# A seven-product output projection: kept weight sums, and the hand-over from attention

## What is computed

```python
B, S, HID = (4, 128, 512)
D, HQ, HK = (128, 32, 8)
Wo = jax.random.normal(ks[4], (HID, HQ * D), jnp.float32) * 0.02
```

## Time and profile before

| what | value |
| --- | --- |
| median of 3 runs | 3381.02 us (3380.08 to 3381.89) |
| the profiled execution | 3377.51 us |
| its span | 3375.7 us, 70348 instructions |
| TensorE busy | 3244.6 us (96%) |
| VectorE, ScalarE, POOL busy | 2498.1, 1839.9, 1649.2 us |
| granted TensorE clock, mean | 0.985 |
| DMA | 647.5 MB, mean 192 GB/s |
| attention | to about 2883.6 us |
| projection | 2888.2 to about 3211.3 us |

### The profile page before, as it was taken

How to read it: one execution, slowest core, us unless ns; L and a number is a source line. 1 busy time by engine, 2 the same in 40 slices (tenths; PEclk the granted TensorE clock), 3 DMA queues, 4 the chain that set the end, 5 groups by cost and what they waited for, 6 DMA issues and landing times. The chain is left out here.

```text
span 3375.7 us, 70348 instructions
## 1 busy us (share of the span) xinstructions
PE 3244.6 (96%) x22206; PEld 2992.9 (89%) x22206; DVE 2498.1 (74%) x6389; ACT 1839.9 (55%) x4523; POOL 1649.2 (49%) x2754
## 2 busy tenths in 40 slices
PE   7799999999899999999899999999999999899899
PEld 5688899987778888888899999999999999788778
DVE  6445544445477777878899999989999998688884
ACT  4323322233227877888666666666666666555432
POOL 0231100000007878788677878767777776055302
PEclk9899999999999999999999999999999999899999
DMA  5412422334545554556776777767777777688753
GB/s 208 136 58 72 126 81 82 86 105 135 198 160 170 178 172 167 186 185 199 244 240 237 243 233 242 238 198 241 241 237 233 240 246 273 215 319 312 252 181 107
DMA packets 401100, 647.50 MB, mean 192 GB/s; under 512 B 41754, under 2 KB 267866, under 8 KB 383835
## 3 DMA queue, kind: packets, MB, share of 16 engines
q1 hardware_dynamic: 381018, 504.58, 44.5%
q0 software_dynamic: 19712, 138.42, 12.6%
HBM read 444.93 MB, written 197.92 MB: 190 GB/s over the span
## 5 line engine op out<-in xcount | busy, mean ns | idle before, releaser
L2657 PE MATMUL l2a_x<-l2a_pt,l2a_V 128*128 128x128 f32 x4096 | 545.0, 276 | 10.9 <-issue 8.9
L2657 PEld LDWEIGHTS l2a_x<-l2a_pt,l2a_V 128*128 128x128 f32 x4096 | 500.2, 193 | 13.5 <-issue 12.7
L2569 DVE CUSTOM_DVE_ANT_0 l2a_sm<-l2a_s,l2a_B 128x544 f32<-128x544 f32 x512 | 366.7, 716 | 63.2 <-PE l2a_s L199 55.6
L2523 ACT ACTIVATE l2a_p<-l2a_sm,l2a_st 128x544 f32<-128x544 f32 x512 | 380.0, 742 | 30.6 <-DVE l2a_st L2569 30.3
L2346 POOL CAST keys<-cache 128x256 fp32r x750 | 302.4, 451 | 184.1 <-issue 175.7
L2508 ACT ACTIVATE l2a_pt<-l2a_t 128x512 f32<-128x512 f32 x512 | 305.5, 597 | 101.1 <-PE l2a_t L2640 97.6
L2346 POOL CAST l2a_K<-cache 128x256 fp32r x768 | 306.8, 448 | 13.9 <-issue 6.3
L2640 PE MATMUL l2a_t<-ident,l2a_p 128*128 128x128 f32 x2048 | 307.7, 273 | 5.2 <-ACT l2a_quads L2516 5.2
L2581 DVE TENSOR_SCALAR l2a_p<-l2a_p,l2a_st 128x512 f32<-128x512 f32 x512 | 295.3, 577 | 18.2
L2069 POOL MEMSET l2q_eps<- 128x5 f32 x1 | 0.1, 103 | 622.8 <-DMA s_x<-moe_xr 622.8
L2516 ACT ACTIVATE l2a_quads<-l2a_x 128x128 f32<-128x128 f32 x512 | 142.0, 277 | 293.2 <-PE l2a_x L2658 293.2
(11 more groups left out here) (1033 smaller groups left out, 9074.0 us busy)
## 6 DMA issues: line engine op xcount, KB each, us to landing
s_qT<-l2q_qo SPq DMA_DIRECT2D x128, 512.0 KB, 2.8
part<-s_ao SPq DMA_DIRECT2D x28, 2048.0 KB, 9.3
head<-s_qT SPq DMA_DIRECT2D x64, 512.0 KB, 6.1
l2a_Q<-s_qT SPq DMA_DIRECT2D x64, 512.0 KB
s_ao<-l2a_combos SPq DMA_DIRECT2D x64, 512.0 KB, 4.5
s_ao<-l2a_quads SPq DMA_DIRECT2D x64, 384.0 KB, 2.5
s_kn<-l2q_ko SPq DMA_DIRECT2D x128, 128.0 KB
head<-s_kn SPq DMA_DIRECT2D x32, 512.0 KB, 5.9
```

The source lines that it names most:

```text
L2523: act.activation(prr[sc % 6][:, :].rearrange("p (k g j) -> p g k j", k=4, j=8), smr[sc % 2][:, :].rearrange("p (g k j) -> p g k j", k=4, j ...
L2569: dve.tensor_tensor_reduce(out=smr[sc % 2][:, :], in0=ps_s[sc % 2][:, 224:768], in1=Br[g % 2][:, :], scale=-SCALE, scalar=3e38, op0=ALU.ad ...
L2657: pe.matmul(px[:, P:256], V[:, k * D + hg * P:k * D + hg * P + P], pt[:, k, :], start=k == 0, stop=False)
```

## The change

Three edits.

**Kept sums.** The sum that POOL makes for product 3, B1 + B2 - B3, is stored by SP to a new buffer `s_wo_sum` in HBM, one store of 128 KB a step (`keep`). Product 6 loads block 0 and that sum, two DMAs of 128 KB, instead of the four blocks, and POOL makes one difference instead of three sums. A raw buffer whose sum is being stored is only loaded anew when the store has landed (`kept`).

**First parts.** The first three parts are asked for in pass `U - 2` of attention's loop instead of `U - 5`.

**Last combinations.** `combine` and `store_combos` are handed to `l2_out`, which makes and stores the last four combinations at its own start. `quads` and `combos` are allocated first in `l2_attn`, and `o` first in `l2_out`, over them. The order of blocks in `quads` is changed, so that one instruction of 128x512 makes t1 and t3 together; `quads` is then stored with two DMAs (two blocks and one).

```diff
@@ l2_attn
+    quads = st.slots("quads", 2, [P, 4, 256], each=2)
+    combos = st.slots("combos", 1, [P, 4, 256])
...
+    def store_combos(sp, k):
+        sp.wait_ge(combined, 3 * k + 3)
+        sp.dma_start(pair_at(k)[:, 3:7, :], combos[k][:, :, :]).then_inc(combos.sem(k), 16)
+
+    def combine(pool, k):
+        q, c = quads[k], combos[k]
+        pool.wait_ge(o_copied, 8 * k + 8)
+        if k:
+            pool.wait_ge(*combos.landed(k - 1))
+        pool.tensor_tensor(c[:, 0:2, :], q[:, 2:4, :], q[:, 1:3, :], ALU.subtract).then_inc(combined, 1)
+        pool.wait_ge(combined, 3 * k + 1)
+        pool.tensor_tensor(c[:, 2, :], q[:, 3, :], c[:, 0, :], ALU.subtract).then_inc(combined, 1)
+        pool.wait_ge(combined, 3 * k + 2)
+        pool.tensor_tensor(c[:, 3, :], q[:, 0, :], c[:, 2, :], ALU.subtract).then_inc(combined, 1)
...
-                    sp.dma_start(pair_at(k)[:, 0:3, :], quads[k][:, 0:3, :]).then_inc(quads.sem(k), 16)
+                    sp.dma_start(pair_at(k)[:, 0:2, :], quads[k][:, 0:2, :]).then_inc(quads.sem(k), 16)
+                    sp.dma_start(pair_at(k)[:, 2, :], quads[k][:, 3, :]).then_inc(quads.sem(k), 16)
...
-                    if sc == U - 5:
+                    if sc == U - 2:
...
-            store_combos(G // 2 - 1)
...
-            combine(G // 2 - 1)
@@ l2_out
-    sums_of = (0, 0, 2, 1, 1, 3, 0)
+    sums_of = (0, 0, 2, 1, 1, 1, 0)
...
                     if s >= 8 + NA:
                         sp.wait_ge(w_lo, s - NA + 1)
-                    a, z = blocks_of[p]
-                    sp.dma_start(raw_of(s), A["wo4"][k, :, a:z, :]).then_inc(raw_in[(s - 8) % NA], 16)
+                        if steps[s - NA][0] == 2:
+                            sp.wait_ge(kept[steps[s - NA][1] % 4], 16 * (steps[s - NA][1] // 4 + 1))
+                    if p == 5:
+                        sp.dma_start(raw_of(s)[:, 0, :], A["wo4"][k, :, 0, :]).then_inc(raw_in[(s - 8) % NA], 16)
+                        sp.dma_start(raw_of(s)[:, 1, :], S["wo_sum"][k]).then_inc(raw_in[(s - 8) % NA], 16)
+                    else:
+                        a, z = blocks_of[p]
+                        sp.dma_start(raw_of(s), A["wo4"][k, :, a:z, :]).then_inc(raw_in[(s - 8) % NA], 16)
+
+            def keep(s):
+                p, k, _ = steps[s]
+                if p == 2:
+                    sp.wait_ge(raw_summed, sums_at[s + 1])
+                    sp.dma_start(S["wo_sum"][k], raw_of(s)[:, 0, :]).then_inc(kept[k % 4], 16)
...
             parts.fetch(sp, 3)
+            store_combos(sp, uses - 1)
             sp.wait_ge(*before_c.landed(uses - 1))
             blocks.fetch(sp)
             for s, (p, k, ns) in enumerate(steps):
+                keep(s)
                 if s >= 8:
                     raw(s + NA)
...
-                    for h in range(2):
-                        sp.wait_ge(d_sems[h][0], 16)
+                    for z in (*d_sems[0], d_sems[1][0]):
+                        sp.wait_ge(z, 16)
...
+            combine(pool, uses - 1)
...
                     if p == 5:
-                        pool.tensor_tensor(r[:, 0, :], r[:, 0, :], r[:, 3, :], ALU.add).then_inc(raw_summed, 1)
-                        pool.tensor_tensor(r[:, 1, :], r[:, 1, :], r[:, 2, :], ALU.add).then_inc(raw_summed, 1)
-                        pool.wait_ge(raw_summed, sums_at[s] + 2)
                         pool.tensor_tensor(r[:, 0, :], r[:, 0, :], r[:, 1, :], ALU.subtract).then_inc(raw_summed, 1)
```

More of the change, by code:

```diff
@@ L2298, in l2_attn @@
     Br = [st.sb(f"B{i}", [P, KV]) for i in range(2)]
-    quads = st.slots("quads", 2, [P, 4, 256])
-    combos = st.slots("combos", 1, [P, 4, 256])
     ps_s = [st.ps(f"s{i}", [P, 1024]) for i in range(2)]
@@ L2356, in l2_attn, with pair_at @@
     fill = {1: 15, 2: 8, 4: 10, U // 2: 30}
+    def pair_at(k):
+        half, m = divmod(k, NB // 2)
+        return S["ao"][half, m // 2, :, :, m % 2, :]
+    def store_combos(sp, k):
[11 more added lines that the diff above has]
+        pool.tensor_tensor(c[:, 3, :], q[:, 0, :], c[:, 2, :], ALU.subtract).then_inc(combined, 1)
     def units(i):
@@ L2391, in fetch_new_values @@
                                  S["vn"][b * 32:(b + 1) * 32, (4 * half + h) * P:(4 * half + h + 1) * P]).then_inc(Nr.sem(g), 16)
-            def pair_at(k):
-                half, m = divmod(k, NB // 2)
-                return S["ao"][half, m // 2, :, :, m % 2, :]
-            def store_combos(k):
-                sp.wait_ge(combined, 4 * k + 4)
-                sp.dma_start(pair_at(k)[:, 3:7, :], combos[k][:, :, :]).then_inc(combos.sem(k), 16)
             sp.dma_start(iota[:, :], A["keypos"]).then_inc(iota_in, 16)
@@ L2455, in values @@
                                         bass.IndirectOffsetOnAxis(ap=rows[:, half, b:b + 1], axis=0)).then_inc(Vr.sem(g), 16)
-            def combine(k):
-                b11, b21, b22, b12 = (quads[k][:, e, :] for e in range(4))
-                t1, t2, t3, t4 = (combos[k][:, e, :] for e in range(4))
-                pool.wait_ge(o_copied, 8 * k + 8)
-                if k:
-                    pool.wait_ge(*combos.landed(k - 1))
-                pool.tensor_tensor(t1, b12, b11, ALU.subtract).then_inc(combined, 1)
-                pool.tensor_tensor(t3, b22, b12, ALU.subtract).then_inc(combined, 1)
-                pool.wait_ge(combined, 4 * k + 1)
-                pool.tensor_tensor(t2, b22, t1, ALU.subtract).then_inc(combined, 1)
-                pool.wait_ge(combined, 4 * k + 3)
-                pool.tensor_tensor(t4, b21, t2, ALU.subtract).then_inc(combined, 1)
             values(0)
@@ L2660, in l2_attn @@
     before.marks.close()
-    S["ao_stores"] = quads, combos, G // 2
+    S["ao_stores"] = quads, combos, G // 2, combine, store_combos
     return st
@@ L2708, in l2_out @@
     st = Stage(nc, "l2o")
+    o = [st.sb(f"o{h}", [P, 2, 2, 16, 2, 32]) for h in (1, 0)][::-1]
     ident, _ = S["ident"]
@@ L2719, in l2_out @@
     raw_in = [st.sem(f"wr{i}") for i in range(NA)]
+    kept = [st.sem(f"kept{i}") for i in range(4)]
     wp = [st.pair(f"w{i}", [P, 256]) for i in range(4)]
     bp = [st.pair(f"b{i}", [P, D]) for i in range(6)]
-    o = [st.sb(f"o{h}", [P, 2, 2, 16, 2, 32]) for h in range(2)]
     dr = st.slots("dr", 3, [P, D])
@@ L2750, in l2_out @@
     ends.update({max(s for s, z in enumerate(steps) if z[0] == p): (p, None) for p in range(1, 6)})
+    landings = [0] * N
+    for s in range(8, N):
+        landings[s] = (landings[s - NA] if s >= 8 + NA else 0) + (32 if steps[s][0] == 5 else 16)
     def raw_of(s):
@@ L3112, in build @@
     S["vn"] = dram("s_vn", (2048, 1024))
+    S["wo_sum"] = dram("s_wo_sum", (16, P, 256))
     S["ao"] = dram("s_ao", (2, NB // 4, P, 7, 2, 256))
```

18 lines of the change are left out of this document (9 added, 9 removed).

## The result

The changed kernel takes 3386.65 us (median of 20 runs, 3381.31 to 3393.68), the one before 3381.99 us in the same jobs (20 runs, 3374.91 to 3383.45). The ratio is 1.0018, with a 95% interval of 1.0011 to 1.0025: 0.18% slower. That is within the 0.2% that the prediction calls no change, but the whole interval lies above 1, and its upper end lies beyond 0.2%. The profiled execution took 3385.95 us, its span is 3384.1 where it was 3375.7, 8.4 us more. This small difference is a sum of terms of up to 32 us with both signs, as the windows show, cut at the stages and products as in the earlier trace rows.

A forecast was written before the change was run, and what follows sets the result against it. TensorE was taken to set the pace, so only what makes its steps late counts; -11.1 - 2.5 - 12.0 + 2.0 + 25.6 + 1.5 = +3.5 us on 3381.02, about 3384.5, range 3371 to 3397.

The forecast's parts named there:

- Attention's end: Last units of attention: `vn` loads ahead of the parts remove the 8.39 us stall; -11.1 us, bounds 8.4 and 13.9.
- Combinations out of the hand-over: Between attention's last copy and the next stage's first load: 4.6 us becomes 2.1; gain 2.5 us.
- Start of the next stage: First matmuls after attention: no gain counted; starting at full clock was only the upper bound, 13.9 us, of attention's gain.
- SyncE late at the start: Product 1, step 15: SyncE waits for the last combinations' store before its loop; +2.0 us, bounds 0 and 5.
- Sixth product: One POOL sum a step instead of three stops slowing VectorE; -12.0 of 12.5 us, bounds 9 and 12.5.
- Keeping: Products 3 and 4: SyncE waits for each store's landing before the next load; +25.6 us, plus 1.5 for half clock.
- The recurrence: Product 3 on: serial loads and stores plus parts make step 63 15.4 us late and step 71 25.6 us late.
- the pair: One raw load plus its store in series: 3.45 us with three blocks, 2.95 with two; bounds 2.75 and 4.45.
- rival 1: SyncE's wait for `kept` in product 3: 1 us more per load and store gives +14, 3398.5; chance 0.34 with helpers.
- Rival 2: Stores aren't held up by the parts ahead in the queue, so only the gains stay: 3357.4 us; chance 0.10.
- Rivals 3 and 4: 3: load and store land in 2.75 us, 3377.7, chance 0.10; 4: V's gather late at attention's end, 3395.6, 0.05.
- Signs: Profile: no 8 us wait; next stage 2874.6; products 1, 2: 43.5, 3: 59, 4: 54, sixth: 44; store waits over 12.

The follow-up runs named there:

- ahead3: The changed kernel with each store of sums issued three steps ahead of the load that waits for it, same queue: 3352.5 us, ratio 0.992.

## Why the prediction was right, and what in it was off

The forecast was no change, 3384.5 us in 3371 to 3397; it came out at 3386.65. That it lies 2 us off is in part luck: keeping cost 5 us more than its term, and attention, the next stage's start and the seventh product gave back some 3.5 that were not forecast or lie where nothing was changed. By the windows, without the first and last row, the change is +6.6 us where the sum gave +3.5, and the bound of no change was 6.8. The mechanism holds in every term, but for a tie between the first two that it left out. Term by term:

- **Attention's end: -11.1, measured -12.8**, of which 1.6 lie ahead of the last units, where nothing was changed. The working holds: `vn` no longer queues behind parts, no wait, full clock. Taking it back brings back 8.1 us of idle.
- **Combinations out of the hand-over: -2.5, measured -1.5.** The two stores of quads took 1.01 and 1.57 us to issue, not 0.38 and 0.45: they stand behind three parts, and the store of combinations ahead of them took 5.2. What the term left out is its tie to the one before. The prediction took the store and the combine for independent of the moved parts; without this edit the hand-over would take 14.4 us, 10.6 more than in ahead3.
- **Start of the next stage: 0, measured -1.2**; its low clock ended sooner. It lay within the bounds.
- **SyncE late at the start: +2.0, measured +1.9** (the gap of 1.7 at step 15). The size was right; by the experiments both the wait and the parts ahead in the queue set it, the queue more.
- **Sixth product: -12.0, measured -11.4.** POOL's sums as the cause are shown by putting them back.
- **Keeping: +25.6 and +1.5, measured 32.1.** The recurrence has the right steps: raw 55 was forecast 13 us late, and went out at 2974.47, which is the forecast 2990.6 less the 16.2 us by which product 3 began earlier. Step 63 was 16.3 us late (forecast 15.4), step 71 29.2 (forecast 25.6). What was off is the pair, 3.75 and 3.33 us instead of 3.45 and 2.95. That made the last load of the chain 3.8 us late against the forecast; the gap at the parts of step 55 was 14.7 us instead of 15.5. The prediction took the landing of a load alone and added 0.35 us for the store's bytes. In the pair the store is issued 0.38 us behind the load and lands 3.3 us after its own issue (2.9 behind two blocks), so the lag of its issue belongs in the sum too. The low clock after the second idle cost 2.9 us instead of 1.5. 3.6 + 1.4 is the 5 us between 27.1 and 32.1. The fixed cost of about 2 us that the prediction cites from the Trainium skill ("DMA: Bandwidth & Descriptors", anatomy of one DMA, a section on DMAs that GpSimd issues) gave 21 alone for the 25.6, an estimate; with 29.2 measured, the trace decides against it.
- **Rivals.** Keeping cost more, as in rival 1, by 5 us and not by 14: 0.30 and 0.38 us a pair, and 1.4 us at the low clock. That takes the profile's sum out of the band and the ratio to its edge. Rival 2 is refuted for SyncE's queue, which is the one of the change: its stores behind parts held it for 13 us. From ScalarE's queue a store did pass the parts, 6.3 us against 13.5. Its time, 3357, is near that of the two kernels in which the landing is out of the chain (3354.3 and 3352.5). Rivals 3 and 4 didn't occur.
- **Signs.** Most were seen, with product 3 at 61.4 us instead of 59, product 4 at 57.8 instead of 54, and the next stage at 2871.2 instead of 2874.6 (the kernel was 4.2 us ahead before the last units). Three were not. Product 1 took 45.6 us, not 43.5; the prediction's own term of 2.0 for SyncE's late start had said so. The longest waits for a store were 9.9 and 9.6 us, not over 12, since of the 13 us from issue to landing 3.4 and 3.5 are the issue itself. POOL was busy 13.5 us in the sixth, not 17.

## What to carry to other kernels

A store that is issued in the loop that loads, and waited for by that loop before it reuses the buffer, puts load, store and landing in series: look for a queue's wait for its own last DMA, at a low share of the DMA engines. Issue the store as soon as its data exist, far enough ahead for the worst landing (here behind 4 MB), or from the engine that already read the data, on a queue that doesn't hold the large transfers. The bytes were free, the order cost 32 us. And when large transfers are moved in a queue, follow every small one that now lands behind them up to who waits for it: one of them stood in a barrier.

## What the runs showed of the hardware

- A load of 384 KB and a store of 128 KB issued 0.4 us behind it land within 0.4 us of each other (3.3 to 3.4 and 3.3 us after their own issue); 128 KB more in the store add 0.5 us.
- Order of issue held within a queue and not between two. Issued behind 4 MB of parts, a store of 128 KB lands after 13.5 us on SyncE's own queue, behind them, and after 6.3 us on ScalarE's, before them. The price of the second queue is 5.3 to 5.9 us in the median, against 3.2 us on SyncE's queue when the wait drains it.
- What stands ahead in a queue holds the issuing engine as well: one DMA of combinations behind three parts took SyncE 5.2 us to issue (2861.30 after, 2865.06 with the combinations back), where it takes 0.36 with nothing ahead, and what stands behind it in SyncE's program is late by that.
- VectorE and POOL hold each other up when both have two inputs in SBUF, and either can lose: VectorE's sum of 128x512 goes from 684 to 1226 ns, or POOL's of 128x256 from 1.18 to 5.39 us.
- Each of the two long idles in products 3 and 4 was followed by half clock for a few us (granted 0.63 from 3022.1 to 3026.4 and 0.58 from 3056.8 to 3064). TensorE's busy time for the same 192 matmuls rose from 43.5 to 46.6 and 47.7 us; of those 7.3 us some 4 were hidden in the second wait, since the delay grew by only 2.9 behind it.
